# One maximum over two units of scores in both attentions, and a shorter split of the maxima

## What is computed

```python
x = x + _L0_xattn_ref(_layernorm(x), ctx, ctx, Wq, bq, Wk, bk, Wv, bv, Wo, bo)
x = x + _L0_ffn_ref(_layernorm(x), ...)
x = x + _L1_xattn_ref(_layernorm(x), ctx, ctx, mask, Wq, Wk, Wv, Wo)
x = x + _L1_ffn_ref(_layernorm(x), ...)

# inside either attention
scores = einsum('bhqd,bhkd->bhqk', q, k) / sqrt(8)
# the second attention also puts -inf where mask == 0 and above the diagonal
probs = softmax(scores)
out = einsum('bhqk,bhkd->bhqd', probs, v) ... @ Wo
```

## Time and profile before

| | |
|---|---|
| time, median of 3 runs | 429.37 us (425.33 to 429.8) |
| the profiled execution | 426.82 us, its span 425.1 us |
| mean granted clock of PE | 0.936 of full speed |
| PE busy | 352.6 us (83%) |
| DVE busy | 287.6 us (68%) |
| ACT busy | 218.4 us (51%) |
| L958, the maxima | 128 instructions, 85.0 us |
| first attention | about 37.5 to 132 us of the span |
| second attention | about 276 to 378 us of the span |

### The profile page before, as it was taken

The page is one execution under the profiler, slowest core; times in us unless marked ns, Lnnn a source line. Parts: engine busy times, 40 slices in busy tenths (PEclk is TensorE's granted clock), DMA queues, the critical chain, the costliest instruction groups (busy, mean ns, idle before and its releaser), DMA issues. The chain is left out here.

```text
span 425.1 us, 10448 instructions
## 1 busy us (share of the span) xinstructions
PE 352.6 (83%) x3416; PEld 255.1 (60%) x3418; DVE 287.6 (68%) x897; ACT 218.4 (51%) x412; POOL 112.3 (26%) x211
## 2 busy tenths in 40 slices
PE   1684789888876999999999999889899889746563
PEld 0452577777763467767767777647676667533342
DVE  6865678898855654483444434487789989657994
ACT  2252256664664664434344443327455665747884
POOL 6335051020212001200100100135456454621332
PEclk9876589998996999999999999969999999996999
DMA  7654964443126000660063010013344432000011
GB/s 205 153 157 113 226 165 140 132 117 110 61 64 215 0 2 0 125 124 2 0 166 95 1 36 0 1 40 96 93 140 116 117 100 73 2 2 0 25 32 44
DMA packets 54100, 34.98 MB, mean 82 GB/s; under 512 B 38744, under 2 KB 46256, under 8 KB 54064
## 3 DMA queue, kind: packets, MB, share of 16 engines
q1 hardware_dynamic: 44032, 31.43, 27.0%
q10 hardware_dynamic: 10032, 3.08, 3.0%
HBM read 24.60 MB, written 9.44 MB: 80 GB/s over the span
## 5 line engine op out<-in xcount | busy, mean ns | idle before, releaser
L1040 ACT ACTIVATE probs<-ps_e 128x512 f32<-128x512 f32 x128 | 74.9, 594 | 53.3 <-PE ps_e L885 49.7
L958 DVE TENSOR_REDUCE neg<-ps_s 128x4 f32<-128x512 f32 x128 | 85.0, 684 | 20.6 <-PE ps_s L868 18.2
L1286 DVE SCALAR_TENSOR_TENSOR x_all<-ps_ym,c_g,x_all 128x128 f32 (+1 forms) x128 | 36.0, 344 | 63.2 <-PE ps_ym L1381 63.0
L1381 PEld LDWEIGHTS ps_ym<-w,hid 128*128 128x128 f32 x512 | 60.8, 192 | 9.2 <-issue 6.7
L868 PE MATMUL ps_s<-k_rows,q_rows 96*128 96x128 bf16 x512 | 54.9, 236 | 8.9 <-DVE neg L958 4.9
L1371 PE MATMUL ps_h<-tok_t,w 128*128 (+1 forms) x128 | 62.3, 610 | 0.0
L1381 PE MATMUL ps_ym<-w,hid 128*128 128x128 f32 x512 | 62.2, 276 | 0.0
L1488 ACT ACTIVATE hid<-ps_h,b 128x512 f32<-128x512 f32 x64 | 43.1, 684 | 35.6 <-PE ps_h L1371 34.2
L868 PEld LDWEIGHTS ps_s<-k_rows,q_rows 96*128 96x128 bf16 x512 | 40.7, 105 | 22.4 <-issue 10.5
L885 PE MATMUL ps_e<-q_rows,k_rows 128*128 128x128 bf16 x512 | 51.5, 226 | 3.2 <-DMA q_rows<-neg_t 2.4
L885 PEld LDWEIGHTS ps_e<-q_rows,k_rows 128*128 128x128 bf16 x512 | 36.3, 101 | 7.0 <-DMA q_rows<-neg_t 3.3
(11 more groups left out here) (202 smaller groups left out, 539.5 us busy)
## 6 DMA issues: line engine op xcount, KB each, us to landing
k_rows<-k_dram SPq DMA_DIRECT2D x32, 144.0 KB
q_rows<-q_dram SPq DMA_DIRECT2D x32, 144.0 KB
k_rows<-k_dram SPq DMA_DIRECT2D x16, 288.0 KB
q_rows<-q_dram SPq DMA_DIRECT2D x16, 288.0 KB
k_dram<-parts SPq DMA_DIRECT2D x35, 128.0 KB, 2.4
w<-in_w SPq DMA_DIRECT2D x16, 128.0 KB, 2.7
q_dram<-parts SPq DMA_DIRECT2D x15, 128.0 KB, 2.2
q_dram<-parts ACTq DMA_DIRECT2D x9, 128.0 KB, 3.0
```

The source lines that it names most:

```text
L958: dve.tensor_reduce(neg[:, s, q * HQ:(q + 1) * HQ], ps_s[:, q % 2, :].rearrange("p (h k) -> p h k", h=HQ), AX_X, ALU.max, negate=True).the ...
L1040: act.activation(probs[:, s, q, :], ps_e[:, q % 2, :], ACT.Exp, scale=SCALE).then_inc(exp_done, 1)
L1286: dve.scalar_tensor_tensor(out=batch_of(x_all, g * G + j), in0=ps_y[:, e % 2, j * D:(j + 1) * D], scalar=c_g[:, j, e:e + 1], in1=batch_of( ...
L1381: last = pe.matmul(ps_y[:, e % 2, j * D:(j + 1) * D], hid[:, (e % 2) * M + m, j * P:(j + 1) * P], w2[:, e, m, :], start=(m == 0), stop=(m ...
```

## The change

Three things change in the attentions, for both layers.

- PE issues the scores of two units in a row, into bank 0 and bank 1, in q = 0 and q = 2 of a step. The first of the two waits until the maxima of the pair before are done.
- DVE takes the maxima of both banks with one instruction (128 x 1024 in, 128 x 8 out), in q = 1 and q = 3. `residual` and its wait move from before the last maximum to behind the split.
- In `split` the second part is computed as difference, rounded to bfloat16 on output, directly from `neg` and the first part. It no longer waits for `neg_rest`; four instructions stay four, with one wait less between them.

```diff
@@ PE, scores(b, q, r)
-                wait(pe, max_done, n - 1)
+                if q % 2 == 0:
+                    wait(pe, max_done, b * 2 + q // 2)
@@ PE, step(b, r)
                 for q in range(NQ):
-                    if exists(b + 2):
+                    if exists(b + 2) and q % 2 == 0:
                         scores(b + 2, q, (r + 2) % SLOTS)
+                        scores(b + 2, q + 1, (r + 2) % SLOTS)
@@ DVE
-            def maxima(b, q, s):
-                n = b * NQ + q
-                wait(dve, scored, n + 1)
-                dve.tensor_reduce(neg[:, s, q * HQ:(q + 1) * HQ], ps_s[:, q % 2, :].rearrange("p (h k) -> p h k", h=HQ),
+            def maxima(b, pair, s):
+                wait(dve, scored, b * NQ + pair * 2 + 2)
+                dve.tensor_reduce(neg[:, s, pair * 2 * HQ:(pair + 1) * 2 * HQ],
+                                  ps_s[:].rearrange("p q (h k) -> p (q h) k", h=HQ),
                                   AX_X, ALU.max, negate=True).then_inc(max_done, 1)
...
-                wait(dve, max_done, (b + 1) * NQ)
+                wait(dve, max_done, b * 2 + 2)
                 ch.step(dve.tensor_copy(neg_parts[:, s, 0:H], neg[:, s, :]))
                 ch.settle()
                 ch.step(dve.tensor_tensor(neg_rest[:, s, :], neg[:, s, :], neg_parts[:, s, 0:H], ALU.subtract))
-                ch.settle()
-                ch.step(dve.tensor_copy(neg_parts[:, s, H:2 * H], neg_rest[:, s, :]))
+                ch.step(dve.tensor_tensor(neg_parts[:, s, H:2 * H], neg[:, s, :], neg_parts[:, s, 0:H], ALU.subtract))
                 ch.settle()
@@ DVE, step(b, r)
-                    if q == 3 and exists(b - 2):
-                        residual(b - 2)
-
-                        wait(dve, x_ready, b - 1)
                     if q == 3 and piece and layer == 0:
                         piece[0](1)
-                    if exists(b + 2):
-                        maxima(b + 2, q, s)
+                    if exists(b + 2) and q % 2 == 1:
+                        maxima(b + 2, q // 2, s)
                         if q == NQ - 1:
                             split(b + 2, s)
                     if q == 3 and exists(b - 2):
+                        residual(b - 2)
+
+                        wait(dve, x_ready, b - 1)
                         stats(b - 2)
```

More of the change, by code:

```diff
@@ L995, in step @@
                 for q in range(NQ):
+                    if q == 3 and piece and layer == 0:
+                        piece[0](1)
+                    if exists(b + 2) and q % 2 == 1:
+                        maxima(b + 2, q // 2, s)
+                        if q == NQ - 1:
+                            split(b + 2, s)
                     if q == 3 and exists(b - 2):
@@ L999, in step @@
                         wait(dve, x_ready, b - 1)
-                    if q == 3 and piece and layer == 0:
-                        piece[0](1)
-                    if exists(b + 2):
-                        maxima(b + 2, q, s)
-                        if q == NQ - 1:
-                            split(b + 2, s)
-                    if q == 3 and exists(b - 2):
                         stats(b - 2)
```

## The result

The changed kernel takes **437.24 us** (median of 4 runs, 435.06 to 437.74), the kernel before, run beside it, 429.59 (425.33 to 430.73). The ratio is **1.0198, 95% interval [1.0145, 1.0251]**. The profiled executions are 426.82 us (span 425.1) and 437.63 (span 435.9).

A forecast was written before the change was run, and what follows sets the result against it. In the attentions neither DVE nor PE was taken as full: the two wait for each other in turn. The stage terms summed to +5.6 us on a base of 428.1, giving 433.7, so 434 us, range 426 to 441.

The forecast's parts named there:

- The ring: Steady step of both attentions: PE and DVE alternate over both banks, 4.92 us in the first, 5.36 in the second.
- The merged instruction: DVE's maximum over both banks: 1.20 us, bounds 1.15 and 1.31, saving about 0.1 us a pair.
- first attention, steps 2 to 5: A step goes from 4.72 to 4.92 us: +0.8 us in all, ends -0.4 and +1.2.
- The split: Both attentions: a gain of 0.11 us per batch; after the last maxima only this counts, -0.2 us.
- First start: First attention, steps -2 to 1: alternation without cover, partly swallowed, +2.3 us, ends 0 and +3.1.
- Second start: Start of the second attention, longer pairs at the lower clock: +3.5 us, ends +1.0 and +4.8.
- Second loop: Second attention, steps 6 to 13: 5.97 us a step, 5.77 before, +1.6 us, ends -0.5 and +3.4.
- The piece of q = 0: Second attention, steps 6 to 13: stands before the first maximum, adding 0.53 us a step in the mean.
- Second attention, steps 2 to 5: Waits for loaded rows partly disappear: a step goes from 6.07 to 5.77 us, -1.2 us, ends -2.8 and 0.
- DVE is the real bound: Rival, both attentions: the waits are swallowed and the kernel gets faster, 424 us; chance 0.15.
- The clock gives way: Rival, attention steps: PE stands still in one piece, five more steps at half clock, +7.5 us, 441; chance 0.12.
- A wash: Rival: starts cost 2.5 us in all, transfers and loads hold first steps anyway; +0.4 us, 428.5; chance 0.2.

The follow-up runs named there:

- e2: The changed kernel with one maximum per bank, back to back, each unit of scores waiting only for its own bank: 423.53 us, ratio 0.987.
- e9: The changed kernel with the old split (second part by a cast of the difference): 440.8 us, ratio 1.027.
- e1: The kernel before with the shorter split alone: 426.33 us, ratio 0.9914.
- e3: The changed kernel with batches 0 to 3 of both attentions unit by unit, pairs from batch 4 on: 427.96 us, ratio 0.9988.
- e10: The changed kernel with batches 0 to 3 unit by unit in the second attention only: 430.71 us, ratio 1.005.
- e5: The changed kernel with the piece of q = 0 moved behind the first pair's maximum in the second attention: 435.02 us, ratio 1.0165.
- e6: The changed kernel with POOL clearing two triangles a step instead of three in the second attention, PE masking the third unit: 434.67 us, ratio 1.0158.
- e11: The kernel before with the shorter split and the residual behind it, scores and maxima unit by unit: 426.26 us, ratio 0.9962.
- e4: The changed kernel with the split's first instruction as an addition of zero instead of a cast: 437.29 us, ratio 1.0206.
- e7: The changed kernel with the residual and its wait back in front of the last maximum, pairs kept: 454.47 us, ratio 1.0593.

## Why the prediction was right, and where its sizes were off

The direction and the mechanism were right, and the median of 437.24 us lies in the range, 3 above the forecast. The ring came out nearly to the number; the sum over the stages less so (+9.1 in the traces, +5.8 forecast), and where it came near, errors of both signs and the clock of the two executions had a share.

- **The ring.** Maximum 1.22 (forecast 1.20), PE's notice 0.15 (0.14), scores to maximum 0.65 (0.71), idle 0.79 (0.85), step 4.88 (4.92). The second attention's first wait in a steady step, 1.40 at 304.09 us, was put at 1.29. e2 shows that this ring is the cause: with a maximum per bank the step is 4.47 and 3.3 points come back.
- **The merged instruction.** Forecast to save 0.1 us a pair; against two maxima in a row (e2) it saved 0.06 (1.28 to 1.22). The ends of the stage "first attention, steps 2 to 5", -0.4 and +1.2, don't follow from the bounds of the pair that the prediction names: 1.15 and 1.31, twice a step, give +0.4 and +1.7.
- **The split.** Forecast 0.11 a batch, 32 batches, 3.5 us, of which the last two batches stood by themselves in the sum. Measured 0.7 to 0.9 points, 3.0 to 3.7 us (e9, e1), and 2.3 by the medians of e1. Right within what can be told.
- **First start.** +1.4 over steps -2 to 1 (forecast +2.3): the half step was 2.42, not 2.58, and steps 0 and 1 swallowed 1.05. The rows put that down to the transfer of the laid maxima: before, the shifted scores of step 1 wait for it on PE, and with them the next scores; DVE is idle 3.57 us there, 2.54 after, where PE's row has no such wait. PE before:

```profile
51.00 0.61 PE L885 MATMUL ps_e<-q_rows,k_rows 128*128 128x128 bf16 x4 [1.73 <-DMA q_rows<-neg_t]
```

- **Second start.** +3.8 in steps -2 and -1, +4.8 with the two behind it (forecast +3.5): the lower clock held for some 7 us longer, on which the forecast had laid only its upper end of +4.8. (That end doubles a pair of 1.15 us to "about 2.1"; twice it is 2.3, and the rows give 1.92, 279.31 to 281.23.) e3 and e10 confirm that the two starts are the largest part of the loss.
- **Second loop.** Forecast 5.97 a step, measured 6.14, +2.96 in all instead of +1.6. The piece of q = 0 on the ring was foreseen (e5). What was missing is POOL: the change moved the split to a time in the step at which POOL is clearing a triangle, and its first instruction is held 0.28 us a step in steps 2 to 5 and 0.35 in the loop. With one triangle less (e6) the loop takes 5.81 a step, below the forecast. This is the term that was mis-sized.
- **Second attention, steps 2 to 5.** Forecast -1.2, measured -0.15; the same hold, four times 0.28. With it gone (e6) the stage takes 23.36 us, -0.90. The scores' wait for rows had vanished as foreseen (at 301.47 DVE waits 0.16).

I had counted for each engine only what it waits for by semaphore. Before, the split fell mostly into POOL's pauses. The warning was in the trace all the same: six of its 128 instructions are longer than 0.18 us (1.25, 0.48, 0.34, 0.31, 0.31 and 0.20), and each ends 0.03 us behind an instruction of POOL.

The rivals. "DVE is the real bound" needed looped steps under 5.0 and 5.75 and got 5.09 and 6.14. "The clock gives way" did not happen where it was put, in the steady work: the stretch at half clock of step 10 went, another of the same 3.4 us came (64 to 67 us). The mean clock fell from 0.936 to 0.922; of the 13.5 us more at the lower level, 6.8 lie at the second start and 10.1 behind step 14 of the second attention. "A wash" needed waits for transfers and loads to hide the starts; they hid 1.05 us of the first.

Open: why two units of scores in a row help (e11 to e2), how much of the loss goes through the granted clock, and beside which instructions of POOL a small one of DVE is held.

## What to carry to other kernels

Two buffers are worth something only as long as each is released by itself: an instruction that reads both at once turns a double buffer into a single one of twice the size, and the fixed cost that it saves (0.06 us a pair here) must be set against producer and consumer taking turns (here 0.2 to 0.5 us a step, and 1.5 to 1.9 where nothing else fills the time, as at the start of a stage). Measure the parts of a change apart, since a small gain (the split) can hide the size of a loss (the pairs). When an edit moves a small vector instruction in time, look in the trace at what GpSimd does at the new time too, though no semaphore joins them. And compare stages of two traces only after a look at the granted clock in each: here a stage with the same code took 9.85 us with no time at the lower level and 11.58 with 4.8 us of it (e10, e3).

## What the runs showed of the hardware that was not expected

- Small DVE instructions that write SBUF from SBUF (16 elements, 0.17 us) lasted until the GpSimd instruction beside them ended: 0.46 us beside a select of 0.63, 2.33 beside an addition of 4.54. That held for a cast and for an addition with two SBUF inputs; a reduction from PSUM kept 1.22 us. Beside GpSimd's `rstd` of 128 x 8 (1.65 us) they kept 0.17.
- In steps -2 to 1 of the second attention PE had 13.6 to 17.1 us at the granted clock of 0.50 in the six traces with pairs there (after, e4, e5, e6, e7, e9; PE waits 1.2 to 1.4 us in each half step of steps -2 and -1 of after) and 3.4 to 13.6 in the eight without. The ranges touch, in e3, so the waits are not the only thing that counts.
- Two reductions of 512 elements in a row took 1.28 us, one of 1024 took 1.22, one of 512 by itself 0.68. An estimate from these: the fixed part of one is 2 x 0.68 - 1.22 = 0.14 us, and of the second one in a row 0.06 of it shows; the rest is overlapped.
